# Attention block on one core: the residual shift moved behind the output stage, x reloaded during the key products, the group-norm chain moved into the score stage

## The reference

```python
B, C, H, W = (16, 512, 32, 32)
h = group_norm(x, gn_w, gn_b)                  # 32 groups, EPS 1e-5
hf = h.reshape(Bx, Cx, N)                      # N = 1024
qkv = jnp.einsum('oc,bcn->bon', qkv_w, hf) + qkv_b[None, :, None]
q, k, v = jnp.split(qkv, 3, axis=1)
attn = softmax(jnp.einsum('bnc,bcm->bnm', q, k) / sqrt(C), axis=-1)
o = jnp.einsum('bnm,bmc->bnc', attn, v)
o = jnp.einsum('oc,bcn->bon', out_w, o) + out_b[None, :, None]
return x + o
```

## Time and profile before

| what | value |
|---|---|
| median of 3 runs | 1984.98 us (1984.97 to 1986.65) |
| the profiled execution's own time | 1984.35 us |
| its span, first to last instruction | 1982.6 us |
| PE busy | 1973.3 us |
| DVE busy | 1667.9 us |
| ACT busy | 1123.0 us |
| POOL busy | 447.9 us |
| mean granted TensorE clock | 0.999 |

### The profile page before, as it was taken

How to read it: one execution, slowest core, us unless ns; L and a number is a source line. 1 busy time by engine, 2 the same in 40 slices (tenths; PEclk the granted TensorE clock), 3 DMA queues, 4 the chain that set the end, 5 groups by cost and what they waited for, 6 DMA issues and landing times.

```text
span 1982.6 us, 26069 instructions
## 1 busy us (share of the span) xinstructions
PE 1973.3 (100%) x9895; PEld 1681.2 (85%) x9895; DVE 1667.9 (84%) x2010; ACT 1123.0 (57%) x1431; POOL 447.9 (23%) x306
## 2 busy tenths in 40 slices
PE   9999999999999999999999999999999999999999
PEld 7888878888888888888888888888888888888888
DVE  8897987969889798797988979788797988969866
ACT  6564636646465564645746466563664646556461
POOL 1112140121412213131131401214022141221311
PEclk9999999999999999999999999999999999999999
DMA  6305143051431604325033240424305143150411
GB/s 177 129 7 130 59 74 119 6 139 49 75 118 16 167 12 75 119 41 153 6 73 116 58 136 6 113 76 74 120 7 143 45 75 118 19 171 4 75 33 54
DMA packets 102636, 157.89 MB, mean 80 GB/s; under 512 B 49376, under 2 KB 51264, under 8 KB 102512
## 3 DMA queue, kind: packets, MB, share of 16 engines
q0 software_dynamic: 31264, 73.15, 17.0%
q1 hardware_dynamic: 71248, 83.08, 13.7%
HBM read 85.57 MB, written 68.26 MB: 78 GB/s over the span
## 4 chain that ended last, share of the span: by engine, by line
PE 91%; DVE 4%; DMA 2%; ACT 1%; issue 1%; POOL 1%; SPq 0%; DVEq 0%; POOLq 0%; ACTq 0%
PE ring L459 30%; PE ring L461 30%; PE ring L460 30%; DMA stage<-stage 1%; DVE r_lo L1289 1%; DMA out<-all_max 0%; DVE stage L1457 0%; POOL stage L1170 0%; DVE h_lo L1264 0%; DVE stage L1524 0%; ACT stage L761 0%; POOL out L1179 0%; DMA stage<-wq 0%; DVE stage L1373 0%; ACT stage L774 0%
## 5 line engine op out<-in xcount | busy, mean ns | idle before, releaser
L459 PE MATMUL ring<-r_hi 128*128 128x512 f32 (+1 forms) x1724 | 656.6, 381 | 0.2 <-DVE r_lo L1477 0.2
L460 PE MATMUL ring<-r_lo,r_hi 128*128 128x512 f32 (+1 forms) x1724 | 656.4, 381 | 0.0
L461 PE MATMUL ring<-r_hi,r_lo 128*128 128x512 f32 (+1 forms) x1724 | 656.2, 381 | 0.0
L459 PEld LDWEIGHTS ring<-r_hi 128*128 128x128 f32 x1724 | 324.2, 188 | 62.2 <-DVE r_lo L1477 0.7
L461 PEld LDWEIGHTS ring<-r_hi,r_lo 128*128 128x128 f32 x1724 | 324.2, 188 | 62.0
L460 PEld LDWEIGHTS ring<-r_lo,r_hi 128*128 128x128 f32 x1724 | 324.2, 188 | 61.4
L881 ACT ACTIVATE stage<-ring,keybias 128x512 f32<-128x512 f32 x256 | 175.2, 685 | 164.3 <-PE ring L461 161.6
L1170 POOL PARTITION_ALL_REDUCE stage<-stage x32 | 127.3, 3977 | 465.8 <-DVE stage L1530 465.8
L854 ACT ACTIVATE stage<-ring,by_tile 128x512 f32<-128x512 f32 x120 | 82.5, 688 | 250.7 <-PE ring L461 250.7
L1462 DVE TENSOR_TENSOR r_lo<-stage,r_hi 128x1024 fp32r<-128x1024 f32 x128 | 182.2, 1453 | 0.0
L1450 DVE TENSOR_TENSOR run_max<-run_max,stage 128x512 f32<-128x512 f32 x192 | 132.0, 694 | 54.1 <-ACT stage L881 49.3
(11 more groups left out here) (199 smaller groups left out, 3979.2 us busy)
## 6 DMA issues: line engine op xcount, KB each, us to landing
xs<-x_in SPq DMA_DIRECT2D x64, 512.0 KB, 5.7
out<-xs SPq DMA_DIRECT2D x60, 512.0 KB, 2.7
out<-run_max POOLq DMA_DIRECT2D x60, 256.0 KB, 5.6
inv<-inv_row SPq DMA_DIRECT2D x32, 256.0 KB, 4.5
out<-spare POOLq DMA_DIRECT2D x30, 256.0 KB, 7.6
out<-all_max POOLq DMA_DIRECT2D x30, 256.0 KB, 5.0
r_hi<-g_dram POOLq DMA_DIRECT2D x15, 512.0 KB, 6.2
r_lo<-g_dram POOLq DMA_DIRECT2D x15, 512.0 KB, 5.5
```

The costliest lines, as they stand in the source:

```text
L459: nc.tensor.matmul(ps_out, st_hi, m_hi, start=first, stop=False, skip_group_check=goes_on)
L460: nc.tensor.matmul(ps_out, st_hi, m_lo, start=False, stop=False, skip_group_check=goes_on)
L461: return nc.tensor.matmul(ps_out, st_lo, m_hi, start=False, stop=last, skip_group_check=goes_on)
```

## The change

`change_input` collects SP's stores and loads of `xs` (same instructions, same place in SP's list). For images after the first, `shift_input` runs at the end of the previous image's list on ACT, behind the last `h_combined_part`, instead of in S. `h_combined_rest(b + 1, 1)`, the low half of t2, goes ahead of the four `scale_output` of nb = 1. The group chain moves forward, for images 1 to 14: `group_variance` stands directly behind the statistics, `group_std_part` between ACT's S2 and S3 copies, `group_root` and `group_spread` ahead of the maxima of nb = 0, `affine_pair` ahead of `subtract_max`. Image 0 keeps its order.

```diff
+            def change_input(b):
+                for k in range(CT):
+                    sp.wait_ge(s_shifted, b * CT + k + 1)
+                    sp.dma_start(out_v[b, :, k, :], xs[:, k, :]).then_inc(s_sent[k], DMA)
+                for k in range(CT):
+                    sp.wait_ge(s_sent[k], (b + 1) * DMA)
+                    sp.dma_start(xs[:, k, :], x_v[b + 1, :, k, :]).then_inc(s_x[k], DMA)
...
# ScalarE
                     copy_scores(b, P_A12, k, k, k, s_c11, CT)
-                    shift_input(b, k)
+                    if b == 0:
+                        shift_input(b, k)
                 act.wait_ge(s_tlo, splits(b + 1))
                 for i in range(CT):
                     copy_scores(b, P_S2, i, i, 8 + i, s_p2)
+                if 0 < b < B - 1:
+                    group_std_part(b + 1)
...
                 for i in range(CT):
                     copy_scores(b, P_A22, i, CT + i, CT + i, s_c21)
-                if b + 1 < B:
+                if b == 0:
                     group_std_part(b + 1)
...
                         h_combined_part(b + 1, c)
+                    for k in range(CT):
+                        shift_input(b + 1, k)
# VectorE
                     for q in range(CT * NB):
                         stats_part(b + 1, q)
+                if b > 0 and more:
+                    group_variance(b + 1)
...
+                if b > 0 and more:
+                    group_root(b + 1)
+                    group_spread(b + 1)
                 for i in range(CT):
                     max_step(b, 0, CT + i, CT + i, s_c21, b * 4 + i + 1)
-                if more:
+                if b == 0:
                     group_variance(b + 1)
                 for i in range(CT):
                     add_scores(b, P_S4, i, 8 + i, s_p2, s_c12)
                     max_step(b, 1, CT + i, i, s_c12, b * 4 + i + 1)
+                if b > 0 and more:
+                    affine_pair(b + 1)
                 for q in range(CT):
                     subtract_max(b, 0, q)
-                if more:
+                if b == 0:
                     group_root(b + 1)
                     group_spread(b + 1)
...
-                    if more:
-                        affine_pair(b + 1)
                     v12_rest(b, 0)
...
                     h_combined_rest(b + 1, 0)
+                    h_combined_rest(b + 1, 1)
                 for c in range(CT if more else CT - 1):
                     scale_output(b, 1, c)
...
-                    for c in range(1, CT):
+                    for c in range(2, CT):
                         h_combined_rest(b + 1, c)
```

More of the change, by code:

```diff
@@ L421, in _ @@
             for b in range(B):
-                for k in range(CT):
-                    if b + 1 < B:
-                        sp.wait_ge(s_shifted, b * CT + k + 1)
-                        sp.dma_start(out_v[b, :, k, :], xs[:, k, :]).then_inc(s_sent[k], DMA)
                 if b + 1 < B:
-                    for k in range(CT):
-                        sp.wait_ge(s_sent[k], (b + 1) * DMA)
-                        sp.dma_start(xs[:, k, :], x_v[b + 1, :, k, :]).then_inc(s_x[k], DMA)
+                    change_input(b)
                     group_stats(b + 1)
@@ L1026, in _ @@
                     copy_scores(b, P_A22, i, CT + i, CT + i, s_c21)
-                if b + 1 < B:
+                if b == 0:
                     group_std_part(b + 1)
-                if b == 0:
                     exponential(b, 0, 0)
```

## The result

| | before | changed |
|---|---|---|
| median | 1985.74 us (4 runs) | 2002.97 us (4 runs, 2001.85 to 2007.13) |
| the profiled execution's own time | 1984.35 us | 2007.13 us |
| its span | 1982.6 us | 2005.3 us |

The ratio is 1.0092, with a 95% interval from 1.0077 to 1.0107: slower by 0.9%, or 17 us. The profiled execution of the changed kernel is the longest of its four, 4 us above their median, so its sums come out that much larger.

A forecast was written before the change was run, and what follows sets the result against it. PE bounds the kernel, busy for all but 9 us of the span. Terms 8.7 + 1.6 + 3.2 - 7.5 = +6.0 on 1984.35 give 1990.4, forecast as a median of 1991 us; range 1985 to 2008.

The forecast's parts named there:

- rival 1: In S, the statistics' load back falls behind the loads of u: 1.9 us for thirteen images, 2012 us; chance 0.17.
- t2's low half: In T, its move ends S2's wait: gain 4.0 us in image 2 and 2.5 in the others, 6.3 with finer figures.
- Shift behind A, x in T: Shift (4.6 us of ACT) fits 10.8 us idle before T's copies; x arrives before the statistics want it; both cost nothing.
- the sum: Over the whole kernel: 8.7 + 1.6 + 3.2 - 7.5 = +6.0 us on the profiled execution's 1984.35.
- Image 1: In S, PE waits 8.7 us (7.5 to 10) for A22, plus 1.6 of slow clock; its 1.2 in V goes.
- Images 2 to 14: In S, PE waits 0.25 us per image (0 to 1.9 by the bounds) before A22, 3.2 us in all.
- images over 122.5: Sign in the image windows: images longer than 122.5 us would mean rival 1.
- Rival 2: In S, the thirteen images wait nothing and only image 1 pays, 7.5 us: +1.6, 1986.6 us; chance 0.22.
- Rival 3: On ACT, a drain of 1.38 us between square root and exponential in 14 images: +19, 2010 us; chance 0.02.
- Rival 4: The moved shift or x transfers delay T, 0.5 us or so per image: +7, 1998 us; chance 0.05.
- Rival 5: Faster, 1980 us: image 1 would have to wait under 4 us in S; chance 0.04.
- Behind the chain: From the end of S to V, subtract_max starts near 951.0 instead of 949.44; cost nothing, with 1 us of cover.

The follow-up runs named there:

- the first experiment: The changed kernel with the whole group chain put back in its old places, the other moves kept: 1977.29 us, ratio 0.9966 to the kernel before.

## Why the prediction was right, and where it was off

The direction and the place held: slower, by PE waiting for the S3 copies behind the square root. The size did not: +6 forecast, +17 measured. 2003 lies between the forecast's 1991 and rival 1's 2012, and inside the range only because the range took in most of rival 1.

- **t2's low half.** Right. The 6.3 us came in full, shown alone; the wait moved nowhere else. The first late output scale still meets S1 in time.
- **Shift behind A, x in T.** Right. ACT's idle time before the first copy of T fell from 10.8 to 7.1 (4.3 us of shift, and the parts of h half a microsecond earlier) and the copy starts as before. The statistics left 38.7 us after the start of T in image 6, as worked out (928.4 less 889.75), and DVE never waits for x. By itself this part wins 3 us, out of the same 7.5 that the sum gives to t2's half and to image 1. The sum let image 1's 1.2 us in V go because DVE and ACT catch up while PE waits; the run with the shift and x alone shows that these two are enough for it, with no wait in S.
- **Image 1.** Right in kind and size: 8.95 us of wait against 8.7, and 2.0 of slow clock against 1.6, 11.1 in all against 10.3. None of it would have been paid later in the kernel anyway: with image 1 in the old order the image was clean.
- **Images 2 to 14: the step that failed.** "Taken: 2.38, to 930.8" and "Load back: 1.7, to 932.5", 0.25 of wait for each, 3.2 in all. The trace shows 18.7. The store was taken from a single row, of image 1, and without loads of u beside it, it takes 2.1 to 3.2. The first load of u starts 2.6 us behind the store's issue (2.35 in image 13). With a longer store the load back is issued behind it, as in seven of the thirteen images, and takes up to 4.2 instead of 1.7. This is rival 1's mechanism, to which I gave 0.17; by the prediction's own sign (images over 122.5), images 5, 6 and 9 are rival 1. I had seen that it was 0.2 us from happening and still priced the term at its good end. With the loads of u out of the way, the thirteen images still lost 6.7 us, about twice the 3.2: that much goes with the store's own length, and the rest of the 18.7 hangs on the loads of u. Over that edge is not a few tenths more: three images paid 3.8 to 5.1 us each, past the 1.9 that I had set as the upper bound, because I had stretched the load alone, where a late store comes with it, and because the clock fell to 1.2 GHz behind their waits of 1.98 to 3.21 us.
- **Rival 2** fell: the margin was not there in seven of the thirteen images, and image 1 waited 8.95 and not 7.5. **Rival 3**: in image 6, the exponential starts 1.52 us behind the square root, after 4.1 us of idle time. The Trainium skill (ScalarE: Activation LUTs, What ACT_TABLE_LOAD costs) would have a drain of 1.38 us beside the load of 1.28; no run here shows one on this switch. **Rival 4** is excluded by the first experiment. **Rival 5**, faster, fell with image 1's wait.
- **Behind the chain.** Nothing was late in V in the changed kernel, as worked out.

Images 5, 6 and 9 of the profiled execution lose more than the others; in the trace with image 1 in the old order it is images 4 to 8. No second trace of the changed kernel was taken. That the uneven images make its spread of 5 us, where the clean versions spread over 1 us or less, is therefore argued. Which images pay goes with how long the store takes: in the profiled execution the three dear ones have the three longest of images 2 to 14 (2.99 to 3.11 us), and the cause of that stays open. The Trainium skill (DMA: Bandwidth & Descriptors, Latency and other measured facts) says that a DMA's access to HBM takes longer under load; the load back beside u agrees (up to 4.2 us, against 1.5 to 1.8 ahead of it). The store, which varies from 2.1 to 3.2 with no load of u in flight, is not explained by it.

## What to carry to other kernels

An instruction that waits for a round trip through DRAM belongs where nothing behind it in its engine's list is due before the trip can end; here the same wait was free one product later in images 2 to 14, and cost 1.4 us an image in its place, 10 us with the data late. When a step is moved to within a few tenths of another queue's start, price it at both sides of that edge, since the delays here were not small on the far side. Take the time of a DMA from all of its rows, and not from one: this store's rows in the kernel before run from 2.4 to 5.6 us over images 1 to 14, and the prediction used two of them. And try a change's parts alone: two changed lines held nearly all of the gain, and the rest of the change hid it.

## What the runs showed that I had not expected

DVE's tiny instructions in `group_root` cost much less in their new place. In the kernel before, the scalar-tensor-tensor on 32x1 took 1.04 us; its start (954.16 in image 7) is that of POOL's reduction over partitions of 1.78 us. In the changed kernel it took 0.21 in images 1 to 14, where no reduction ran beside it; in image 0, in its old place and again at the start of a reduction (104.19), it took 1.04. The group rows of the 15 instructions, before and then after:

```profile
L1572 DVE SCALAR_TENSOR_TENSOR by_group<-by_group 32x1 f32<-32x1 f32 x15 | 15.6, 1043 | 0.5
```
```profile
L1579 DVE SCALAR_TENSOR_TENSOR by_group<-by_group 32x1 f32<-32x1 f32 x15 | 3.9, 262 | 0.5
```

That it is the reduction that stretches it is only argued, from the equal starts; no run was made for it. It lies off the path of PE here.

The clock, too, is not a matter of the wait's length alone. Behind the wait of 1.98 us in the earlier trace rows it fell to 1.2 GHz, and so it did behind the four longest of the changed kernel (1.98 to 8.95 us). In the run with image 1 in the old order it fell behind a wait of 1.82 us in image 4, but PE waited 2.06 us in image 7, and the next matmuls start at the usual 0.23 us. Its timeline of PE:

```profile
940.76 0.47 PE L462 MATMUL ring<-r_hi 128*128 128x512 f32 x1 [2.06 <-ACT stage L884]
941.07 0.40 PE L463 MATMUL ring<-r_lo,r_hi 128*128 128x512 f32 x1
941.30 0.40 PE L464 MATMUL ring<-r_hi,r_lo 128*128 128x512 f32 x1
```
